# Attention with a routed MLP: low halves of context and K formed in PSUM by TensorE, V kept once in fp32, more of P's low halves on GpSimd

## The reference

```python
x = x + tanh(g_xattn[0]) * xattn(layernorm(x), ctx_768, mask, Wq, Wk, Wv, Wo)
# xattn, 16 heads of 16 columns:
q = x @ Wq;  k = context @ Wk;  v = context @ Wv
attn = softmax(mask(q @ k.T * hd ** -0.5))
out = (attn @ v) @ Wo
x = x + tanh(g_ffn[0]) * moe(layernorm(x), ...)      # top 2 of 8 experts
```

## Time and profile before

| | |
|---|---|
| time, median of 3 runs | 675.3 us (672.08 to 678.09) |
| profiled execution, span from first to last instruction | 669.9 us |
| what lies around that span, against the median | 5.4 us |
| PE busy | 489.1 us (73%) |
| DVE busy | 441.8 us (66%) |
| ACT busy | 317.2 us (47%) |
| POOL busy | 272.3 us (41%) |

### The profile page before, as it was taken

How to read it: one execution, slowest core, us unless ns; L and a number is a source line. 1 busy time by engine, 2 the same in 40 slices (tenths; PEclk the granted TensorE clock), 3 DMA queues, 4 the chain that set the end, 5 groups by cost and what they waited for, 6 DMA issues and landing times. The chain is left out here.

```text
span 669.9 us, 14994 instructions
## 1 busy us (share of the span) xinstructions
PE 489.1 (73%) x4678; PEld 441.9 (66%) x4679; DVE 441.8 (66%) x920; ACT 317.2 (47%) x566; POOL 272.3 (41%) x244
## 2 busy tenths in 40 slices
PE   3378578998899999899988300008999999999910
PEld 2367477887888888788867200006999999999810
DVE  1755378786888988899988598603555555555417
ACT  1332355664657767667656542504444444444301
POOL 9302255552454455554545158860222222222223
PEclk9688699897999999999989655557999999999965
DMA  8438566677788868877420547823121222221038
GB/s 182 130 95 232 129 154 158 161 230 204 180 233 230 219 187 207 240 187 190 124 49 3 201 159 243 290 81 126 54 62 61 63 63 63 63 63 48 33 99 261
DMA packets 82169, 96.43 MB, mean 144 GB/s; under 512 B 27240, under 2 KB 67648, under 8 KB 82000
## 3 DMA queue, kind: packets, MB, share of 16 engines
q1 hardware_dynamic: 78576, 86.71, 47.5%
q0 software_dynamic: 3552, 9.19, 3.9%
HBM read 62.80 MB, written 32.96 MB: 143 GB/s over the span
## 5 line engine op out<-in xcount | busy, mean ns | idle before, releaser
L346 POOL TENSOR_TENSOR PL<-PT 125x448 f16<-125x448 f32 x96 | 100.2, 1046 | 145.8 <-ACT PT L468 145.7
L732 DVE TENSOR_REDUCE mx<-bank 112x1 f32<-112x375 f32 x256 | 130.7, 542 | 43.2 <-PE bank L566 41.0
L468 ACT ACTIVATE PT<-bank 125x448 f32<-125x448 f32 x192 | 103.8, 544 | 91.7 <-PE bank L581 91.2
L1277 POOL DMA_INDIRECT y_scr<-ys,where x42 | 40.3, 959 | 153.1 <-DVE ys L1387 146.7
L566 PE MATMUL bank<-KS,QS 97*112 97x376 f32 x256 | 90.0, 374 | 13.9 <-DVE mx L732 11.4
L581 PE MATMUL bank<-QS,KS 98*125 98x256 f32 x384 | 84.0, 304 | 14.6 <-DMA QS<-nm 13.3
L1375 DVE SCALAR_TENSOR_TENSOR hf<-bank,ub,sg 128x256 f32<-128x256 f32 x84 | 39.2, 483 | 62.9 <-ACT sg L1299 62.9
L581 PEld LDWEIGHTS bank<-QS,KS 98*125 98x125 f32 x384 | 66.7, 193 | 16.6 <-DMA QS<-nm 9.7
L1299 ACT ACTIVATE sg<-bank,gb,inv 128x256 f32<-128x256 f32 x84 | 42.8, 560 | 73.4 <-PE bank L1334 73.4
L1334 PE MATMUL bank<-xH,GH 128*128 128x256 f16 x336 | 64.9, 275 | 0.8 <-DVE xL L1367 0.5
L1334 PE MATMUL bank<-xL,GH 128*128 128x256 f16 x336 | 64.9, 275 | 0.0
(11 more groups left out here) (203 smaller groups left out, 1110.2 us busy)
## 6 DMA issues: line engine op xcount, KB each, us to landing
KS<-k_scr SPq DMA_DIRECT2D x48, 376.0 KB
k_scr<-kH SPq DMA_DIRECT2D x16, 376.0 KB, 2.8
k_scr<-kL SPq DMA_DIRECT2D x16, 376.0 KB, 3.7
xs_scr<-empty SPq DMA_DIRECT2D x9, 642.5 KB, 9.1
xt<-xs_scr SPq DMA_DIRECT2D x21, 257.0 KB
QS<-q_scr SPq DMA_DIRECT2D x96, 56.0 KB, 5.0
ctx_sb<-in_ctx SPq DMA_DIRECT2D x16, 281.2 KB
wsq<-in_L_ffn_gate_w SPq DMA_DIRECT2D x8, 512.0 KB, 4.6
```

What stands on the lines that cost most here:

```text
L346: pool.tensor_tensor(PL[:, 2 * k:2 * k + 2, :, 0:N], PT[:, 2 * k:2 * k + 2, :, 0:N], PH[:, 2 * k:2 * k + 2, :, 0:N], ALU.subtract).then_in ...
L468: act.activation(PT[:, 2 * k:2 * k + 2, :, 0:N].rearrange("p a e i -> p (a e) i"), psST[k % 2][0:JP].rearrange("p (a i) -> p a i", i=NI)[: ...
L732: dve.tensor_reduce(mx[:, hd:hd + 1], psS[hd % 2][0:N, 0:M], AX.X, ALU.max).then_inc(v_max, 1)
L1277: pool.indirect_dma_start(y_scr, bass.IndirectOffsetOnAxis(ap=where[:, t % UN, k:k + 1].bitcast(mybir.dt.uint32), axis=0), ys[:, u, k, :], ...
```

## The change

- **Low parts by TensorE.** After `kH` has been copied out, `k_rest` adds minus `kH` (a matmul with a negated identity, `minus`) onto the projection that still stands in `misc`, in slot 4 behind `sums(0)`. ScalarE then copies `misc` to `kL` behind its exp of slot 4. `ctx_rest` in slot 12 and ScalarE's `transposed_low` in slot 13 do the same for `cTL`. VectorE's two subtractions go. `project_v`, and SyncE's write of `kH` and `kL`, now wait for ScalarE's copy.
- **V once.** `VS` is fp32 and V is copied from `misc` straight into it; GpSimd forms the second and third part in fp32, in slots 12 and 13 of the same trip. The matmul reads the upper halves of the words in place (`VT`), so its moving operand steps by 4 bytes. ScalarE's two copies per trip go.
- **P's low parts.** GpSimd does nine of the twelve, VectorE k = 4, 8 and 11.
- The V projection stands in slots 5, 6, 7. `qH` and `qL` have two buffers where they had four, so `q_high(2)` and `q_high(3)` wait for the writes of groups 0 and 1.

```diff
-        VS = sb("VS", [JP, NB, JT, HEADS, VW], BF16)
+        VS = sb("VS", [JP, NB, JT, HEADS, VW], F32)
+        VT = VS[:].rearrange("p u t h w -> p (u t h w)").bitcast(BF16).rearrange(
+            "p (u t h w two) -> p u t h w two", u=NB, t=JT, h=HEADS, two=2)[:, :, :, :, :, 1]
+        minus = sb("minus_ident", [128, 128], F32R)
...
-        vf = sb("vf", [JP, NB, JT, DIM], F32)
...
-        qH = first("qH", [128, GROUPS, 2, GB * N], F32R)
-        qL = first("qL", [128, GROUPS, 2, GB * N], F32R)
+        qH = first("qH", [128, 2, 2, GB * N], F32R)
+        qL = first("qL", [128, 2, 2, GB * N], F32R)
...
-        vr = sb("vr", [JP, JT, DIM], F32)
...
-        POOL = [k for k in (1, 2, 3, 5, 6, 8) if k < SB]
+        POOL = [k for k in range(SB) if k not in (4, 8, 11)]
...
-        VP = (4, 5, 6)
+        KR, VP = 4, (5, 6, 7)
         ST, AG, XC, XT, LG, RT = 5, 14, 7, 11, 12, 13
 
-        V1, VR, V2, LV = 3, 3, 6, 6
+        VR, LV, CR = 12, 13, 12
...
-                    sp.wait_ge(v_K, b + 1)
+                    sp.wait_ge(a_KL, b + 1)
...
-                    b, h, u = at(i, c - 1)
-                    part = lambda k: VS[:, u, :, :, HD * k:HD * (k + 1)]
-                    head = lambda t: t[:].rearrange("p t (h d) -> p t h d", d=HD)
-                    pool.wait_ge(a_V1, b + 1)
-                    wait(pool, g_V, b)
-                    pool.tensor_tensor(head(vr), vf[:, u].rearrange("p t (h d) -> p t h d", d=HD), part(0), ALU.subtract).then_inc(g_r, 1)
+                    b, h, u = at(i, c)
+                    flat = lambda t, k: t[:, :, :, HD * k:HD * (k + 1)].rearrange("p t h d -> p (t h) d")
+                    pool.wait_ge(a_V, b + 1)
+                    pool.tensor_tensor(flat(VS[:, u], 1), flat(VS[:, u], 0), flat(VT[:, u], 0), ALU.subtract
+                                       ).then_inc(g_r, 1)
 
                 def last_values(i, c):
-                    b, h, u = at(i, c - 1)
-                    part = lambda k: VS[:, u, :, :, HD * k:HD * (k + 1)]
-                    head = lambda t: t[:].rearrange("p t (h d) -> p t h d", d=HD)
-                    pool.wait_ge(a_V2, b + 1)
-                    pool.tensor_tensor(part(2), head(vr), part(1), ALU.subtract).then_inc(g_V, 1)
+                    b, h, u = at(i, c)
+                    flat = lambda t, k: t[:, :, :, HD * k:HD * (k + 1)].rearrange("p t h d -> p (t h) d")
+                    pool.wait_ge(g_r, b + 1)
+                    pool.tensor_tensor(flat(VS[:, u], 2), flat(VS[:, u], 1), flat(VT[:, u], 1), ALU.subtract
+                                       ).then_inc(g_V, 1)
...
+                for k in (values, last_values):
+                    k(0, 0)
...
+                def transposed_low(i, c):
+                    b, h, u = at(i, c)
+                    act.wait_ge(p_Tr, b + 1)
+                    act.activation(cTL[:, :, 0:M], misc[0:CK].rearrange("p (c n) -> p c n", c=2)[:, :, 0:M],
+                                   ACT.Copy).then_inc(a_TL, 1)
...
-                        if k == V2 and live(i, c, 1):
-                            b, h, u = at(i, c - 1)
-                            act.wait_ge(g_r, b + 1)
-                            act.activation(VS[:, u, :, :, HD:2 * HD].rearrange("p t h d -> p (t h) d"),
-                                           vr[:].rearrange("p t (h d) -> p (t h) d", d=HD), ACT.Copy).then_inc(a_V2, 1)
...
+                        if k == CR + 1 and live(i, c, -1) and not starts(i, c):
+                            transposed_low(i, c + 1)
...
-                        if k == V1 and live(i, c, 1):
-                            b, h, u = at(i, c - 1)
-                            act.wait_ge(a_V, b + 1)
-                            wait(act, p_PV, PAIRS * (b - NB + 1))
-                            act.activation(VS[:, u, :, :, 0:HD].rearrange("p t h d -> p (t h) d"),
-                                           vf[:, u].rearrange("p t (h d) -> p (t h) d", d=HD), ACT.Copy).then_inc(a_V1, 1)
...
+                        if k == KR and live(i, c, 0):
+                            b, h, u = at(i, c)
+                            act.wait_ge(p_Kr, b + 1)
+                            act.activation(kL[:, u], misc[:].rearrange("p (m n) -> p m n", m=2)[:, :, 0:MP],
+                                           ACT.Copy).then_inc(a_KL, 1)
...
-                            wait(act, g_r, b - NB + 1)
-                            act.activation(vf[:, u].rearrange("p t n -> p (t n)"), misc[0:JP, 0:JT * DIM], ACT.Copy
+                            wait(act, p_PV, PAIRS * (b - NB + 1))
+                            act.activation(VS[:, u, :, :, 0:HD].rearrange("p t h d -> p (t h) d"),
+                                           misc[0:JP, 0:JT * DIM].rearrange("p (x d) -> p x d", d=HD), ACT.Copy
...
+                    if g >= 2:
+                        act.wait_ge(s_qw[g - 2], 64)
...
-                            mm = pe.transpose(misc[0:CK, 512 * k + JP * t:512 * k + JP * (t + 1)],
-                                              ctx_sb[:, u, t, CK * k:CK * (k + 1)], ident[0:JP, 0:JP])
+                            mm = pe.matmul(misc[0:CK, 512 * k + JP * t:512 * k + JP * (t + 1)],
+                                           ctx_sb[:, u, t, CK * k:CK * (k + 1)], ident[0:JP, 0:JP],
+                                           start=(t == 0), stop=False, is_transpose=True, skip_group_check=True)
...
+                def ctx_rest(i, c):
+                    b, h, u = at(i, c)
+                    pe.wait_ge(a_T, b + 1)
+                    if isinstance(b, int) and b == 0:
+                        pe.wait_ge(s_clear, 2)
+                    for k in range(2):
+                        mm = pe.matmul(misc[0:CK, 512 * k:512 * k + MP], minus[0:CK, 0:CK], cTH[:, k, :],
+                                       start=False, stop=True, skip_group_check=True)
+                    mm.then_inc(p_Tr, 1)
+
+                def k_rest(i, c):
+                    b, h, u = at(i, c)
+                    pe.wait_ge(a_K, b + 1)
+                    for m in range(2):
+                        mm = pe.matmul(misc[:, 512 * m:512 * m + MP], minus[:], kH[:, u, m, :],
+                                       start=False, stop=True, skip_group_check=True)
+                    mm.then_inc(p_Kr, 1)
...
-                        pe.wait_ge(v_T, b + 1)
+                        pe.wait_ge(a_TL, b + 1)
...
-                        pe.wait_ge(v_K, b + 1)
+                        pe.wait_ge(a_KL, b + 1)
...
-                                               VS[:, u, t, hd, :], start=(part == 0 and t == 0),
+                                               VT[:, u, t, hd, :], start=(part == 0 and t == 0),
...
+                        if s == KR and live(i, c, 0):
+                            k_rest(i, c)
...
+                        if s == CR and live(i, c, -1) and not starts(i, c):
+                            ctx_rest(i, c + 1)
...
-                def transposed(i, c):
-                    b, h, u = at(i, c)
-                    dve.wait_ge(a_T, b + 1)
-                    dve.tensor_tensor(cTL[:, :, 0:M], misc[0:CK].rearrange("p (c n) -> p c n", c=2)[:, :, 0:M],
-                                      f32(cTH[:, :, 0:M]), ALU.subtract).then_inc(v_T, 1)
...
-                        if s == KP[-1] + 1 and live(i, c, 0):
-                            b, h, u = at(i, c)
-                            dve.wait_ge(a_K, b + 1)
-                            dve.tensor_tensor(kL[:, u], misc[:].rearrange("p (m n) -> p m n", m=2)[:, :, 0:MP],
-                                              f32(kH[:, u]), ALU.subtract).then_inc(v_K, 1)
```

More of the change, by code:

```diff
@@ L174, in attention @@
         p_T, p_K, p_V, p_S, p_mT = (sem(n) for n in ("pe_ctxT", "pe_k", "pe_v", "pe_scores", "pe_maxT"))
+        p_Tr, p_Kr, a_neg = sem("pe_ctxT_rest"), sem("pe_k_rest"), sem("act_minus_ident")
         p_ST, p_PV, p_OT, p_Wo = (sem(n) for n in ("pe_scoresT", "pe_pv", "pe_oT", "pe_wo"))
[L176 to L177 removed]
+        a_T, a_K, a_V, a_E, a_O = (sem(n) for n in ("act_ctxT", "act_k", "act_v", "act_exp", "act_oT"))
+        a_TL, a_KL = sem("act_ctxT_low"), sem("act_k_low")
+        v_L, v_max, v_nm = (sem(n) for n in ("dve_plow", "dve_max", "dve_negmax"))
         v_os, v_rd, v_on, v_O, v_x1 = (sem(n) for n in ("dve_osum", "dve_rden", "dve_on", "dve_oT", "dve_x1"))
@@ L388, in step @@
                 def step(i, c):
+                    if starts(i, c):
+                        return
                     for k in range(SLOTS):
@@ L391, in step @@
                             low(i, c, k)
-                        if k == VR and live(i, c, 1):
+                        if k == VR and live(i, c, 0):
                             values(i, c)
-                        if k == LV and live(i, c, 1):
+                        if k == LV and live(i, c, 0):
                             last_values(i, c)
+                for k in (values, last_values):
+                    k(0, 0)
                 steps(pool, step)
@@ L542, in project_k @@
```

(8 more changed lines are left out.)

17 lines of the change are left out of this document (8 added, 9 removed).

## The result

The changed kernel took 700.4 us (median of 4, 700.28 to 704.2), the kernel before beside it 676.7 us (4, 672.1 to 680.4). The ratio is 1.043, interval 1.038 to 1.048. The forecast was 697 us.

What follows compares the result with a forecast made beforehand. The prediction took the ring through DRAM, set by when `kL` is ready, as the bound. 7.0 + 17.6 - 3.5 (spare time) - 3.3 + 2.7 - 0.9 + 2.0 = +21.6 us on 675.3 gave 697 us, range 679 to 715.

Steps and rivals of the forecast that it cites:

- The ring: `scores_T`, K projection, `kH`, `kL`, write, `KS`, `nm`, next `scores_T`: `nm` lands about 7.8 us after `KS` is issued.
- Six trips without squares, +7.0: `kL` on ScalarE is done 1.16 us later in each of these six trips: +7.0 us.
- Eight squaring trips, +17.6: `kL`, behind the squares and an exp on ScalarE, comes 2.2 us later in each of eight trips: +17.6 us.
- Backlog of the writes, -3.3: Later K writes in squaring trips meet emptier queues; half of 6.5 us excess comes back: -3.3 us (bounds 0 and -6.5).
- Clock in the trips, +2.0: New TensorE waits bring one more cold stretch, half hidden: +2.0 us.
- Rival B: The clock falls in most squaring trips, 22 us in place of 2.0: 717 us; chance 0.13.
- Ahead of the trips, +2.7: Before the trips, `q_high(3)` waits for group 1's write and new matmuls and copies lengthen the chain: +2.7 us (1.8 to 4).
- The last trips, -0.9: Three `low` fewer on VectorE in one trip, -1.5; nine `low` on GpSimd in the final one, +0.6: together -0.9 us.
- Rival A: `nm` doesn't hang on `KS` and lands soon after its own issue; only TensorE counts: +6.5, 682 us; chance 0.14.
- C: VectorE was the bound, so waits for `nm` and TensorE's idle time go: faster, 669 us; chance 0.08.
- D: `VT`'s 4-byte step costs double, so TensorE needs 19.8 us in every trip: +9, 706 us; chance 0.05.
- VectorE under 13 us busy: Sign that the forecast is right: VectorE busy under 13 us in a trip, from 15.82 in a trip without squares.

Runs made afterwards that it cites:

- sp_late: The kernel before, with SyncE's write of `kH` and `kL` held back until TensorE has done the first third of the V projection; 690.9 us, ratio 1.024.
- split_after: The changed kernel, with SyncE writing `kH` once ready and loading its copies when that write has landed, then dealing with `kL`; 677.3 us, ratio 1.005.
- kl_dve: The changed kernel, with VectorE making `kL` in slot 3 again, no `k_rest`, and the V projection in slots 4 to 6; 675.5 us, ratio 1.002.
- split_before: The kernel before, with the same edit of SyncE's K writes and loads as split_after; 666.3 us, ratio 0.985.
- best1: split_after, with ScalarE's squares moved behind the copy to `kL` in slot 4; 670.3 us, ratio 0.999.
- kl_split: kl_dve, with SyncE's K writes and loads split as in split_after; 668.9 us, ratio 0.993.
- low_split: split_before, with nine low parts of P on GpSimd instead of six; 666.6 us, ratio 0.981.
- both v10: kl_split and best1, each with VectorE taking P's low part of slot 10 and GpSimd that of slot 11; 663.5 us (0.975) and 663.9 us (0.976).
- low_only: The kernel before, with nine low parts of P on GpSimd instead of six; 674.0 us, ratio 1.001.

## Why the prediction was right, point by point

- **The ring** (`nm` lands a fixed time after the `KS` load, so a later `kL` makes a longer trip) held: 7.55 to 8.9 us in every trip of the change, and sp_late and split_after moved only that path, kl_dve little else, and they moved the time by 16, 23 and 25 us.
- **Six trips without squares, +7.0:** trips at full clock 18.5 to 18.7 (forecast 18.3); `kL` at 7.22, 1.27 us later.
- **Eight squaring trips, +17.6:** as forecast in the three that ran at full clock, `kL` at 8.0 to 8.3, trips 19.4 to 19.8. The four with a cold stretch had `kL` at 9.6 to 9.9.
- **Backlog of the writes, -3.3:** mis-sized. From the write to the `KS` load it was 3.54 to 3.61 us in all eight; before it was 3.58 to 5.24, in sum 6.9 us over 3.57. All of it came back, not half: 3.6 us too little taken off.
- **Clock in the trips, +2.0:** mis-sized as well. With the backlog as measured the other terms make 7.0 + 17.6 - 3.5 - 6.9 = 14.2 us of the 19.1, which leaves some 5 us that came with the 8 us more at half clock. `kL` was late by 30 us in sum over the fourteen trips, where the two terms on it make 24.6. The granted clock fell from 0.96 to 0.95 on average. Rival B, a fall in most squaring trips, came in part: in four of eight (two before), after waits on `nm` of only 0.6 to 0.9 us at the start of the trip.
- These terms with the spare time were +19.8 for the fourteen trips; 19.1 were measured. That they agree so well is luck: an error of 3.6 us on the backlog and one of some 3 on the clock cancel.
- **Ahead of the trips, +2.7:** 1.4 was measured, below the lower bound of 1.8.
- **The last trips, -0.9:** this step failed; they took 7.2 us more. Windows of the last two trips, before, then after:

```profile
341.83:356.67 14.84, 12.68 (x158) 10.22 (x154) 14.15 (x33) 9.25 (x20) 9.60 (x8) 1.00 0.01 2
356.67:374.50 17.83, 12.73 (x161) 10.16 (x156) 10.51 (x27) 10.18 (x30) 6.32 (x7) 0.93 0.01 1
```

```profile
362.33:380.96 18.63, 18.24 (x152) 15.97 (x152) 13.30 (x28) 7.93 (x18) 9.15 (x10) 0.55 0.01 2
380.96:402.15 21.19, 16.39 (x159) 14.07 (x155) 9.22 (x22) 10.39 (x29) 8.59 (x9) 0.66 0.00 1
```

  The same matmuls at 1.2 GHz for most of the time in place of 2.4. Ahead of it TensorE had waited, by its timeline:

```profile
362.33 0.51 PE L616 MATMUL bank<-QS,KS 98*125 98x256 f32 x2 [1.68 <-DMA QS<-nm]
```

  The prediction counted instructions there and left the clock out. The wait on `nm` isn't what it hangs on: in eight runs (split_before, split_after, sp_late, best1, kl_split, low_split and both v10) the same trip began with no wait on `nm`, and was granted 0.50 to 0.65 all the same. Windows view of that trip in split_before:

```profile
336.20:355.69 19.49, 19.38 (x157) 16.95 (x153) 14.68 (x33) 9.48 (x20) 10.92 (x8) 0.50 0.01 2
```

  All eight had TensorE wait 1.5 to 1.8 us for a maximum within 8 us of the start of this trip. But so had the kernel before (1.47 us at 335.61) and low_only, which kept full clock in it; kl_dve, with a wait of 1.57 us on `nm`, had 0.79. The two trips took 32.7 us in the trace of the kernel before and 34.6 to 41.3 in the twelve others, so part of the 7.2 us may be a lucky execution there. What decides it stays open.
- **The sum.** +21.6 us were forecast and 28.6 separate the spans: the backlog took off 3.6 more, the clock added some 3, ahead of the trips it was 1.3 less, in the last trips 8.1 more, behind them 1.0 more. From the median of 675.3 to that of 700.4 it is 25.1 only, because the profiled execution before was a short one: its span and the 1.8 us that lie around the span of the changed kernel make 671.7 us, and the prediction added 5.4. That 697 came so near 700.4 owes 3.6 us to this.
- **Rival A** falls by sp_late. The Trainium skill, page "DMA: Bandwidth & Descriptors", section "Anatomy of one DMA — SWDGE (gpsimd) path", which it draws on, gives its fixed cost for transfers issued from GpSimd, not from SyncE. By the trace `nm` did land within 1.8 us once less stood ahead of it (split_before, issued at 293.70). **C** (VectorE was the bound) falls by low_only and low_split; **D** (a 4-byte step costs double) by L635, 191 ns a matmul.
- **"VectorE under 13 us busy"** was a miss: 14.3. The removed subtractions were worth 3.7 us (three low parts, `kL`, the context), and VectorE's busy time fell by 1.4. Of the missing 2.3 us the slow low part is 1.1 and the two products `on` (0.49 us, before 0.29, in such a trip) 0.4; the remaining 0.8 is overlap: the records of VectorE in a trip without squares add up to 17.8 us before and 15.6 now, so 0.8 us of those that went had lain over their neighbours.

## What to carry to other kernels

Before moving work off a busy engine, find the wait that ends last in a trip and follow it back across engines and queues: here a copy of 0.8 us that came 1.2 to 2.3 us later cost some 25 us, the clock's part included. Three low parts fewer on VectorE and two copies of V fewer on ScalarE bought nothing under the ring, and with the ring cut no more than the intervals can tell (0.975, against 0.981 and 0.985). This ring through DRAM was cut by sending each half when it is ready, and not by another queue for the last small transfer. When two engines take turns on one kind of work, look at the single durations of a group, not at its mean; the best version here (0.975) differs from a slower one (0.993) in one number of a table.

## What the hardware showed that was not expected

- A subtraction of two SBUF operands on VectorE that began 0.2 to 0.3 us into GpSimd's own took 1.66 to 1.72 us in place of 0.60 to 0.63, and ended 0.5 us after GpSimd's. Moved by one slot, VectorE's low parts took 0.63 on average. The product `on` took 1.28 us in place of 0.29 once, beside GpSimd's 1.47. When two low parts began within 0.1 us of each other, in the kernel before, VectorE's took its usual 0.62 and GpSimd's up to 1.47 in place of 0.93. The Trainium skill, page "SBUF — State Buffer", section "SBUF: two separate sides", says that the two engines share a pair of ports as an exclusive lock, which whichever starts first holds for its whole instruction; it counts a VectorE instruction with two SBUF inputs against a GpSimd one that reads SBUF. These rows agree.
- 7 KB took 1.8 or 2.8 us to land with `KS` loaded in two steps, 5.4 us behind all of it at once, and 6.9 us with two weight loads ahead of it too.
- A wait can be of use to others: SyncE's wait for `nm` held back over 2 MB of other transfers.
- At the end of the attention's trips most traces show half clock for 10 us and more although TensorE is busy; no run here says what sets it off.
